# Reordering a head's turn: attention blocks moved around the next head's scores, and the division moved behind two marks

## The reference, cut to what matters

```python
draft = einsum('bhqd,bhkd->bhqk', qr, kr) + causal        # 1024 x 1024 for each of 32 heads
_, draft_indices = top_k(draft, 128)                      # exact: 128 per row
mask = neg everywhere, 0.0 at draft_indices, neg in the causal future
attn = softmax(draft / sqrt(16) + mask)
out = attn @ v                                            # then the output projection
```

## Time and profile before

| what | value |
|---|---|
| time before, 3 runs | 3249.15, 3250.77 (median), 3252.75 us |
| the profiled execution | 3250.62 us, span 3248.7 us |
| busy over the span | PE 90%, DVE 76%, ACT 61%, POOL 51%, PEld 55% |
| attention heads, first to last count | 2071 to 3080 us |
| its steady part (26 heads) | 2182.6 to 2999.0 us |
| mean granted TensorE clock, whole span | 0.938 of full speed |

### The profile page before, as it was taken

One profiled execution on the slowest core, in us unless ns is written; L12 is line 12 of the kernel. 1 busy time (PEld: TensorE's weight loads), 2 busy tenths in 40 slices (PEclk: granted clock), 3 DMA queues, 4 the chain that ended last, 5 costly groups with the idle time before them and its releaser, 6 DMA issues. The chain is left out here.

```text
span 3248.7 us, 50391 instructions
## 1 busy us (share of the span) xinstructions
PE 2916.7 (90%) x15823; PEld 1785.8 (55%) x15929; DVE 2466.6 (76%) x4628; ACT 1982.2 (61%) x4218; POOL 1650.4 (51%) x3659
## 2 busy tenths in 40 slices
PE   8999999999999999999999998567888878888879
PEld 4455455454554554554645545346666666666654
DVE  5677697696796876976967877578888888888746
ACT  2464564564554545545645433599999999899723
POOL 3235254263362452542633655677676767677503
PEclk9999999999999999999999999668889898888879
DMA  2222132232231222322321210000000000000010
GB/s 93 59 81 94 66 104 72 75 120 79 72 107 69 88 88 72 104 76 76 112 76 61 89 35 27 1 1 2 2 2 1 2 1 2 2 1 2 2 50 27
DMA packets 65803, 169.62 MB, mean 52 GB/s; under 512 B 11776, under 2 KB 19328, under 8 KB 64512
## 3 DMA queue, kind: packets, MB, share of 16 engines
q1 hardware_dynamic: 54448, 115.17, 10.9%
q10 hardware_dynamic: 11088, 51.19, 4.5%
HBM read 161.08 MB, written 5.24 MB: 51 GB/s over the span
## 5 line engine op out<-in xcount | busy, mean ns | idle before, releaser
L2052 ACT ACTIVATE X<-ah_z,ah_trial 128x256 bf16<-128x256 f32 (+6 forms) x896 | 732.0, 822 | 25.1 <-POOL ah_trial L2155 14.1
L1207 ACT ACTIVATE m_mix<-m_mix,m_cs 128x128 f32<-128x128 f32 x1024 | 312.9, 388 | 255.5 <-DMA m_mix<-cs_rows 255.3
L2007 PE MATMUL ah_ps_o<-a_v,X 128*128 128x17 f32 x2304 | 353.0, 281 | 0.3 <-DVE hT L2252 0.3
L2007 PEld LDWEIGHTS ah_ps_o<-a_v,X 128*128 128x128 f32 x2304 | 339.0, 221 | 0.6 <-issue 0.6
L1089 POOL TENSOR_TENSOR m_xdec<-m_xdt,m_decay_out 128x512 f32<-128x512 f32 x112 | 142.0, 1267 | 213.7 <-DVE m_xdt L1333 202.1
L1117 POOL TENSOR_TENSOR m_squares<-m_squares 128x256 f32<-128x256 f32 x128 | 107.3, 839 | 273.4 <-ACT m_squares L1219 273.4
L2063 ACT ACTIVATE X<-ah_ps_e 128x512 f32<-128x512 f32 (+3 forms) x384 | 184.4, 481 | 94.2 <-PE ah_ps_e L1994 61.4
L1013 PE MATMUL m_ps_x<-m_w_out,m_gate 128*128 128x512 f32 x512 | 233.7, 599 | 0.0
L1013 PE MATMUL m_ps_d<-m_w_out,m_gate 128*128 128x512 f32 x512 | 233.5, 599 | 0.0
L2237 DVE MAX8 ah_top<-ah_ps_m 128x8 f32<-128x256 f32 (+6 forms) x224 | 185.5, 828 | 38.4 <-PE ah_ps_m L1957 34.8
L2224 DVE TENSOR_SCALAR_CACHE_REDUCE X<-ah_z,ah_cut 128x256 bf16<-128x256 f32 (+6 forms) x224 | 193.4, 874 | 22.9 <-POOL ah_cut L2160 22.9
(11 more groups left out here) (319 smaller groups left out, 7578.1 us busy)
## 6 DMA issues: line engine op xcount, KB each, us to landing
m_mix<-cs_rows SPq DMA_DIRECT2D x128, 512.0 KB, 4.4
m_w_proj<-in_w_proj ACTq DMA_DIRECT2D x69, 512.0 KB, 3.3
m_fade<-fade_rows SPq DMA_DIRECT2D x224, 128.0 KB, 2.9
m_w_out<-in_w_out ACTq DMA_DIRECT2D x7, 2048.0 KB, 7.8
X<-in_x SPq DMA_DIRECT2D x8, 256.0 KB, 5.0
m_w_out<-in_w_out SPq DMA_DIRECT2D x1, 2048.0 KB, 10.0
x_away<-X SPq DMA_DIRECT2D x1, 2048.0 KB, 7.3
X<-x_away SPq DMA_DIRECT2D x8, 256.0 KB, 6.2
```

The source lines that it names most:

```text
L1207: act.activation(mix[:, u % 3, h, :], mix[:, u % 3, h, :], ACT.Relu, bias=cs[:, c, h0 + h:h0 + h + 1], scale=-1.0).then_inc(lag_done, 1)
L2007: last = pe.matmul(ps_o[:, t, :], eT[:, g % 3, b * P:(b + 1) * P], v[:, b0 + b, h // REP, :], start=i == 0 and b == 0, stop=b0 + b == t, s ...
L2052: act.activation(sign[:, at % 2, 0:(t + 1) * P], z[:, h % RING, cols(t)], ACT.Sign, bias=trial[:, h % RING, 0, t - 1:t], scale=-1.0, accum ...
```

## The change: what it does

Three edits in two lists of one iteration:

1. PE: chunk 0 of head `n-3` (with `add_v` of chunk 10 of head `n-4`) moves from behind `scores(n+1, 0)` and `sample(n+1)` to ahead of them.
2. PE: chunk 2 of head `n-3` (with `add_v` of its own chunk 0, which waits for `divide(n-4)`) moves from ahead of `marked_scores(n-2, 1)` to behind `scores(n+1, 1)`, just ahead of chunk 3. The order of the chunks among themselves stays.
3. DVE: `divide(n-4)` moves from ahead of `take(n-2, 1)` and `take(n-2, 2)` to behind both, ahead of `pick(n-2, 1)`.

No instruction is added or removed, and no wait either; ACT's, POOL's and SP's lists are untouched.

```diff
-    CHUNKS_FIRST = (0, 1, 2)
+    CHUNK_AHEAD = (0,)
+    CHUNKS_FIRST = (1,)
     CHUNKS_AFTER_MARKED = ((), (), (), (), (), (7,), (9,), ())
-    CHUNKS_AFTER_SCORES = ((), (3,), (4,), (5,), (6,), (8,), (10,), (11,))
+    CHUNKS_AFTER_SCORES = ((), (2, 3), (4,), (5,), (6,), (8,), (10,), (11,))
...
             for n in range(FIRST, LAST):
+                if live(n - 3):
+                    turn_and_add(n - 3, CHUNK_AHEAD)
                 if live(n + 1):
                     scores(n + 1, 0)
                     sample(n + 1)
...
                     add_sample(n + 1)
-                if live(n - 4):
-                    divide(n - 4)
                 if live(n - 2):
                     take(n - 2, 1)
                     take(n - 2, 2)
+                if live(n - 4):
+                    divide(n - 4)
```

## The result

Six runs of the changed kernel: median 3239.06 us (3232.62 to 3243.93), against 3251.76 us (3249.07 to 3256.96) for six of the kernel before. The ratio is 0.9954, 95% interval 0.9941 to 0.9967: faster by 0.46%, 12.7 us between the medians and 15 us by the ratio, where 58 were forecast. The sign was right, the size wrong, and the time lies outside the range of 3175 to 3225 us. The profiled execution took 3232.62 us, span 3230.7; it is the fastest of the six, so differences between profiles flatter the change by about 5 us.

What follows compares the result with a forecast made beforehand. Waits between engines bound the kernel, with DVE's needless division stall at the turn; once gone, ACT binds. 26 heads x (31.40 - 29.2) = 57 us plus about 1 us, off 3250.6, gave 3193 us; range 3175 to 3225 us.

Steps and rivals of the forecast that it cites:

- The stall and what it hid: At DVE's division: 3.0 us a head waiting for PE's products; with the division behind the takes, take 1 gains up to 3.14 us.
- Chunk 0 at no cost: On PE ahead of the next first scores: chunk 0's 1.1 us fits under PE's 2.00 us idle gap, cost nothing.
- the chained sum: Over two heads: ACT's 28.58 us plus a 29.8 us path through cut, takes and row copy, 58.4 us, so 29.2 a head.
- ACT's 28.58 us of work after the previous row copy: On ACT, from one row copy to the end of the next last count: its busy time per head, 28.58 us.
- So DVE would stand 0.9 us there: At DVE's MAX8 of tile 2: marked scores 2 come late behind chunks 2 and 3, so DVE waits 0.9 us a head.
- the bound of 1.8: At DVE's MAX8 of tile 2: upper bound of the wait, about 1.8 us, with all PE work there at low clock.
- the fourth rival: On PE: low clock outlasts the turn and PE is late everywhere; 2.0 us a head slower, 3303 us; chance 0.06.
- The second rival: At the turn: low clock holds, marked scores 2 and chunks come late, ACT waits; 30.0 to 31.0 us a head; chance 0.14.
- The first rival: At the turn: clock stays up, ACT alone binds; 28.58 to 28.8 us a head, 3177 to 3182 us; chance 0.22.
- ACT's floor of 28.58 us: On ACT over the steady heads: a head can't take less than ACT's own busy time, 28.58 us.

Runs made afterwards that it cites:

- the changed kernel with the gaps filled: Changed kernel plus overwritten filler matmuls on PE, 4 ahead of the next head's first scores, 3 each ahead of marked scores 5 to 7: 3192.4 us, 0.9809 of the kernel before.

## Why the prediction was right and wrong

- **The stall and what it hid: right in the mechanism.** The division's wait went to zero, and the take starts at the cut (0.8 us a head of waiting; 1 to 2 were forecast).
- **Chunk 0 at no cost: right, and undervalued.** It fitted under the gap, which fell to 0.96 us. By itself it gives 1.7%; the prediction gave it no term at all and put the gain down to the division. Shown by the runs with one edit each: the division alone +0.17%, chunk 0 alone -1.7%.
- **The step that failed: the chained sum, 28.58 + 29.8 = 58.4 us for two heads.** The same stretches, averaged over the 26 heads of the changed kernel's trace, are: from a row copy to the end of ACT's next last count 30.16 us, from there to the cut 5.0, from take 1 to the row copy 26.1; together 61.3, or 30.65 a head. So two terms were too small, by 1.6 and by 1.3 us.
  - **"ACT's 28.58 us of work after the previous row copy"** has no wait in it. ACT's waits at the exponentials were put at nothing without a reason: in the kernel before, the same stretch took 30.70 us. They stayed at 1.7 us a head (22.0 + 21.6 us in 26 heads); the prediction wanted all of ACT's waits under 20 us, and they are 56.7.
  - **"So DVE would stand 0.9 us there"** measured 1.7 us at tile 2, near the bound of 1.8, and another 0.5 us at tiles 3 and 4, for which there was no term. 0.9 was the middle between clock up and clock down. Part of the miss is the one turn that was read: from marked scores 1 to 2 PE took 2.36 us there and 2.80 on average.
- **The clock: the forecast was wrong.** I let chunk 0 in the gap shorten the low clock; low-clock time rose from 7.5 to 9.2 us a head. Both terms hang on it: in the changed kernel with the gaps filled (3192.4 us) the two stretches are 28.3 and 24.2 us; with 5.4 us to the cut that makes 58.0 for two heads, 29.0 a head. The long heads at clock 0.76 are the fourth rival's mechanism, in about one head of five and not in all.
- **The bound.** Even with 1.8 us at MAX8 the sum gave only 29.65 us a head, 3212 us at the top of the forecast's own span. The second rival had the mechanism: "1.8 us at MAX8 and as much again from chunks late at ACT" measured 1.7 and 1.7 us a head, its 30.0 to 31.0 us a head holds the 30.65, and its 3203 to 3240 us holds the 3239. It had a chance of 0.14, and the stated range took in only its lower part. The first rival, clock up and ACT alone at 28.58 to 28.8 us a head, was not met even with the gaps filled: 29.0 us and 3192.4 where it said 3177 to 3182.
- **The three edits together.** By the ratios, edit 3 beside edit 1 costs about 35 us and edit 2 beside edit 1 about 42; with both the cost is about 40, much the same as with one of them. With edits 1 and 3 PE stood 1.2 us a head at L2008 for the division, ahead of marked scores 1; in the full change that wait is gone from the list, since chunk 2 stands behind them.
- **ACT's floor of 28.58 us: right.** Four kernels keep ACT busy 97 to 98% of the window, and the heads of three of them, taken from their traces, last 28.8 to 29.0 us.

Open: what decides whether the low clock lasts 3, 7 or 17 us after a turn, and what the change is worth with the clock up. The combination of edits 2 and 3 without 1 was not run.

## What to carry to other kernels

A stall names who waits, not what is late: before moving the waiting instruction, shorten what it waits for, and run each edit by itself, since here one of three held all the gain and the others gave most of it back. An engine's queue position is a cost to everything behind it: a chunk taken off one tight path was put on the next one, where the smallest tile has the least slack. When a sum chains the busy time of an engine that does wait, give its waits a term: measure the stretch from end to end over many heads, not in one turn. And where TensorE's granted clock drops at the same place in each loop, price its queue there at the low clock throughout, and try cheap work in the gap first, no longer than the gap.

## What the runs showed that I had not expected

Filler matmuls that compute nothing of use, 4 of 128x512 per head in one gap, made the changed kernel 1.5% faster, with the clock at 0.95 instead of 0.85. A PE wait of 0.96 us at a turn was followed by 1.2 GHz for 7 or 17 us in two of the three turns shown, and in the third by full clock until a second wait of 1.29 us; waits of 1.0 us in mid-head were followed by no drop (clock 1.00 from 2462.2 to 2485 us). So at about 1 us the length of one wait does not tell whether the clock drops.
